# Cross-attention and feed-forward on one core: another order for tiles 4 and 5, a bias row fetched ahead, and an opening that works in smaller pieces

## The reference

```python
def fake_quant(x, s, z):
    q = jnp.clip(jnp.round(x / s + z), 0.0, 255.0)
    return (q - z) * s
x = x + jnp.matmul(fake_quant(_layernorm(x), s1, z1), fake_quant(ctx, s2, z2))
y = _layernorm(x)
base = jnp.matmul(y, w) + bias
A_eff = einsum('bn,nri->bri', gate, lora_A); B_eff = einsum('bn,nor->bor', gate, lora_B)
x = x + base + (y A_eff^T) B_eff^T + (y A_shared^T) B_shared^T
```

## Time and profile before

| what | value |
|---|---|
| runs | 1049.28, 1049.54 and 4784.78 us, median 1049.54 |
| profiled execution | 1046.42 us, its span 1044.9 us |
| PE busy | 991.1 us, 95% of the span |
| DVE, ACT, POOL busy | 536.2, 297.0, 209.8 us |
| granted TensorE clock, mean | 0.996 |
| first product of PE | 15.1 us after the start |

### The profile page before, as it was taken

The page is one execution under the profiler, slowest core; times in us unless marked ns, Lnnn a source line. Parts: engine busy times, 40 slices in busy tenths (PEclk is TensorE's granted clock), DMA queues, the critical chain, the costliest instruction groups (busy, mean ns, idle before and its releaser), DMA issues.

```text
span 1044.9 us, 12005 instructions
## 1 busy us (share of the span) xinstructions
PE 991.1 (95%) x4663; PEld 460.3 (44%) x4663; DVE 536.2 (51%) x756; ACT 297.0 (28%) x213; POOL 209.8 (20%) x233
## 2 busy tenths in 40 slices
PE   2898999898999999999999999998999999999996
PEld 1343444353544444444444444444554444444442
DVE  7766858968554565553423765877542032014010
ACT  4663422253131142232214521363230021012000
POOL 3001100021113013212411643320104004004010
PEclk9999999999999999999999999999999999999999
DMA  8699982859655346446699851767824024014010
GB/s 364 240 307 380 355 306 39 186 115 216 172 183 198 123 152 200 158 149 206 233 294 284 323 204 71 160 123 151 211 107 156 31 101 161 20 40 150 10 50 20
DMA packets 139863, 181.43 MB, mean 174 GB/s; under 512 B 112688, under 2 KB 112688, under 8 KB 127280
## 3 DMA queue, kind: packets, MB, share of 16 engines
q1 hardware_dynamic: 125040, 117.99, 39.1%
q0 software_dynamic: 13632, 58.73, 15.5%
q10 hardware_dynamic: 1152, 4.19, 1.0%
HBM read 124.26 MB, written 29.36 MB: 147 GB/s over the span
## 4 chain that ended last, share of the span: by engine, by line
PE 71%; DVE 10%; DMA 6%; ACT 5%; issue 4%; SPq 1%; POOL 1%; POOLq 0%; ACTq 0%; DVEq 0%
PE psum L1005 17%; PE psum L1187 16%; PE psum L1188 16%; PE psum L1189 16%; PE psum L1210 2%; DVE ring L1446 2%; DMA stage<-in_ctx_in 1%; PE psum L1067 1%; DVE hl L1492 1%; ACT ring L785 1%; DMA bias_sb<-in_bias 1%; DMA xn<-in_x 1%; DMA stage<-in_w 1%; PE psum L1199 1%; PE psum L1198 1%
## 5 line engine op out<-in xcount | busy, mean ns | idle before, releaser
L1187 PE MATMUL psum<-ring,lhs 128*128 128x512 f16 x1016 | 385.8, 380 | 12.6 <-issue 8.5
L1188 PE MATMUL psum<-ring,lhs 128*128 128x512 f16 x1016 | 385.8, 380 | 0.0
L1189 PE MATMUL psum<-ring,lhs 128*128 128x512 f16 x1016 | 385.6, 380 | 0.0
L1005 PE MATMUL psum<-ring,lhs 128*128 128x512 bf16 x1024 | 227.8, 381 | 3.6 <-DVE ring L1412 2.1
L1187 PEld LDWEIGHTS psum<-ring,lhs 128*128 128x128 f16 x1016 | 99.5, 98 | 135.2 <-issue 11.0
L1005 PEld LDWEIGHTS psum<-ring,lhs 128*128 128x128 bf16 x1024 | 100.3, 98 | 126.0 <-issue 4.2
L1189 PEld LDWEIGHTS psum<-ring,lhs 128*128 128x128 f16 x1016 | 99.6, 98 | 120.3 <-issue 0.8
L1188 PEld LDWEIGHTS psum<-ring,lhs 128*128 128x128 f16 x1016 | 99.5, 98 | 118.5 <-issue 0.5
L1499 DVE SCALAR_TENSOR_TENSOR x<-psum,sc,x 128x512 f32<-128x512 f32 (+1 forms) x64 | 45.2, 746 | 191.2 <-PE psum L1199 190.4
L649 POOL TENSOR_TENSOR x<-x,bias_sb 128x512 f32<-128x512 f32 (+1 forms) x64 | 86.6, 1377 | 190.9 <-ACT x L916 130.4
L785 ACT ACTIVATE ring<-stage,sc 128x2048 f16<-128x2048 f32 x32 | 63.6, 1999 | 170.1 <-PE psum L1189 137.8
(11 more groups left out here) (168 smaller groups left out, 656.5 us busy)
## 6 DMA issues: line engine op xcount, KB each, us to landing
stage<-in_w SPq DMA_DIRECT2D x38, 1024.0 KB, 6.3
stage<-in_ctx_in SPq DMA_DIRECT2D x30, 1024.0 KB, 8.1
out<-x POOLq DMA_DIRECT2D x64, 256.0 KB, 3.2
x<-in_x POOLq DMA_DIRECT2D x8, 1024.0 KB, 11.9
xn<-in_x POOLq DMA_DIRECT2D x8, 1024.0 KB, 6.8
x<-in_x POOLq DMA_DIRECT2D x4, 2048.0 KB, 14.7
lhs<-in_lora_a POOLq DMA_DIRECT2D x4, 1024.0 KB, 12.0
lhs<-in_lora_b SPq DMA_DIRECT2D x4, 1024.0 KB, 9.7
```

The lines of the kernel that those rows point to most:

```text
L1005: last = pe.matmul(psum[:, t, :], lhs_q[:, k, t * P:(t + 1) * P], ring_q[:, g, j % 2, u, :], start=(k == 0), stop=(k == KT - 1 and not by_pe))
L1187: pe.matmul(psum[:, t, :], hi, ring[:, g, 0, u, :], start=(kk == 0), stop=False)
L1188: pe.matmul(psum[:, t, :], hi, ring[:, g, 1, u, :], start=False, stop=False)
L1189: last = pe.matmul(psum[:, t, :], lo, ring[:, g, 0, u, :], start=False, stop=False)
```

## The change

In the opening:
- tile 0 of `x` is loaded in two halves with a semaphore each, DVE takes its statistics after each half, ACT scales it in two halves and DVE clips it in two, and PE may turn the first half before the second is clipped;
- group 0 of `ctx` is loaded by POOL between tiles 1 and 2 of `x`, no longer by SP;
- tiles 2 and 3 get their scale one by one (`scale_row`, five DVE instructions, one less than before), where they were a pair;
- the lists of DVE, ACT and PE are written anew: PE starts group 0 of tile 0 before it turns tile 1, and the first column term comes after tile 5, no longer after tile 4.

In the second phase, block 0:
- SP transposes both parts of tile 1 ahead of the load of group 2 of `w`;
- PE takes the products with the high part of group 2 of `w` for tiles 0 and 1 first (`top_group`), which need ACT's work alone, and then the rest (`rest_group`); ACT converts group 2 ahead of the root of tile 2;
- `product_p(b, 0)` and the two `b_pair` stand in front of tile 5, no longer of tile 4, on DVE and ACT; SP transposes tile 5 ahead of `load_a(b, 2)`.

The bias: each block's row is loaded at the end of the addition before it.

```diff
-            load_ctx(0, 0, [0, 1])
+            load_ctx(0, 0, [1])
...
-                        turn_high(b, 1)
-                    if g == 2 and isinstance(j, int) and j == 0:
-                        turn_low(b, 1)
+                        turn_y(b, 1)
...
                 if b == 0:
                     w_peaks_block(1)
+                turn_y(b, 5)
                 load_a(b, 2)
-                turn_y(b, 5)
...
-            load_x(range(4))
+            pool.dma_start(x2[:, 0, 0:D // 2], x_tile[0, 0, :, 0:D // 2]).then_inc(x_half, 16)
+            pool.dma_start(x2[:, 0, D // 2:D], x_tile[0, 0, :, D // 2:D]).then_inc(x_in[0], 16)
+            load_x([1])
+            pool.dma_start(stage[:, 0, :, :], ctx_v[0, 0, 0]).then_inc(first_in, 16)
+            load_x([2, 3])
...
             load_x(range(4, TILES))
-            root_pair(1)
+            root_one(2)
+            root_one(3)
...
+            def next_bias(j, bb):
+                pool.wait_ge(biased, (bb + 1) * TILES)
+                pool.sem_inc(go, 1)
+                pool.dma_start(bias_sb[:, :], bias_row[:, bass.ds(j * NW + NW, NW)].to_broadcast([P, NW])).then_inc(bias_in, 16)
...
                     add_bias(b, j, j + blk2(b, 0), True)
+                    next_bias(j, j + blk2(b, 0))
...
-            relu_rows(0)
-            relu_rows(1)
+            relu_half(0)
+            relu_half(1)
             turn_out(0, range(2))
             ctx_block(0, 0, [0])
+            relu_rows(1)
+            ctx_block(0, 0, [1])
             turn_out(1, range(2))
-            ctx_block(0, 0, [1])
             relu_rows(2)
+            conv_head(2)
             relu_rows(3)
             turn_out(2, [0])
-            conv_head(2)
+            conv_head(3)
             turn_out(3, [0])
-            conv_head(3)
...
+                w_groups(b, 0, [2])
                 root(b, 1, 2)
-                w_groups(b, 0, [2, 3])
+                w_groups(b, 0, [3])
...
                 norm2_rows(3)
+                norm2_rows(4)
                 product_p(b, 0)
                 b_groups(b, 0)
...
             def first_block():
                 turn(0)
+                ring_ready(0, 0, 0)
+                tile_start(0, 0, 0)
+                group1(0, 0, 0, True)
                 turn(1)
+                ring_ready(0, 0, 1)
+                group1(0, 0, 1, True)
+                tile_start(0, 0, 1)
+                for g in range(2):
+                    group1(0, 1, g, True)
                 turn(2)
+                ring_ready(0, 0, 2)
+                for t in range(2):
+                    group1(0, t, 2, True)
+                tile_start(0, 0, 2)
+                for g in range(3):
+                    group1(0, 2, g, True)
                 turn(3)
+                tile_start(0, 0, 3)
+                for g in range(3):
+                    group1(0, 3, g, True)
+                ring_ready(0, 0, 3)
+                for t in range(PT):
+                    group1(0, t, 3, True)
...
# DVE's list of the opening, new
+            stats1(0, range(2)); stats1(0, range(2, NBLK)); variance([0]); scale_row(0)
+            stats1(1, range(2)); round_half(0); stats1(1, [2]); round_half(1); stats1(1, [3]); variance([1])
+            stats1(2, range(2)); scale_row(1); stats1(2, range(2, NBLK)); ctx_group(0, 0, 0); variance([2])
+            round1(1); stats1(3, range(2)); ctx_group(0, 0, 1); scale_row(2); stats1(3, range(2, NBLK)); variance([3])
+            round1(2); scale_row(3); head_group(2); stats1(4, range(1)); turn_out(2); round1(3)
+            stats1(4, range(1, NBLK)); head_group(3); turn_out(3); stats1(5); variance([4, 5])
             scale_rows([4, 5]); stats1(6, range(2)); round1(4); ...
...
                 for t in range(3, TILES):
-                    if t == 4:
+                    if t == 5:
                         product_p(b, 0)
                         for h in range(2):
                             b_pair(b, 0, h)
```

More of the change, by code:

```diff
@@ L682, in _ @@
                     largest(4, MX_W, PW_W)
+                next_bias(0, blk2(b, 0))
                 store(b, 0, blk(b, 1, 0))
@@ L1172, in high_group, with top_group, rest_group @@
                     pe.matmul(psum[:, t, :], hi, ring[:, g, 0, u, :], start=(kk == 0), stop=False)
+                    pe.matmul(psum[:, t, :], hi, ring[:, g, 1, u, :], start=False, stop=False)
+            def top_group(t, g):
+                for u in range(GU):
+                    for h in range(2):
+                        y = lhs[:, h, g * GU + u, t * P:(t + 1) * P]
+                        pe.matmul(psum[:, t, :], y, ring[:, g, 0, u, :], start=False, stop=False)
+            def rest_group(t, g):
+                for u in range(GU):
+                    hi = lhs[:, 0, g * GU + u, t * P:(t + 1) * P]
                     pe.matmul(psum[:, t, :], hi, ring[:, g, 1, u, :], start=False, stop=False)
@@ L1244, in base0_pair @@
                     base_group(1, 1)
[L1245 to L1248 removed]
+                    pe.wait_ge(act_conv, act_w(b, 0, 2) + 1)
+                    for t in range(2):
+                        top_group(t, 2)
+                    pe.wait_ge(converted, grp_w(b, 0, 2) + 1)
+                    for t in range(2):
+                        rest_group(t, 2)
+                    pe.wait_ge(converted, grp_w(b, 0, 3) + 1)
+                    for t in range(2):
+                        base_group(t, 3)
                 def base0(t):
@@ L1354, in stats1 @@
             def stats1(t, parts=range(NBLK)):
-                dve.wait_ge(x_in[t], 16)
+                if t == 0 and 0 in parts:
+                    dve.wait_ge(x_half, 16)
+                else:
+                    dve.wait_ge(x_in[t], 16)
                 for c in parts:
@@ L1382, in scale_rows, with scale_row, round_half @@
                 dve.wait_ge(normed, n + 1)
+            def scale_row(t):
+                i = t % 2
+                root, veps, t2, scale, shift = [v[:, i:i + 1] for v in (
+                    ROOT2, VEPS2, T2, pair_cols(SCALE1, t // 2), pair_cols(SHIFT1, t // 2))]
+                dve.wait_ge(pair_var, t + 1)
+                dve.wait_ge(pair_root, t + 1)
+                then(dve.scalar_tensor_tensor(out=t2, in0=root, scalar=root, in1=veps, op0=ALU.mult, op1=ALU.mult))
+                then(dve.tensor_scalar(t2, t2, 0.5, -1.5, ALU.mult, ALU.add))
+                then(dve.scalar_tensor_tensor(out=t2, in0=root, scalar=IS1, in1=t2, op0=ALU.mult, op1=ALU.mult))
+                dve.tensor_scalar(scale, t2, -1.0, None, ALU.mult)
+                dve.tensor_scalar(shift, MV2[:, i:i + 1, 0], t2, Z1, ALU.mult, ALU.add).then_inc(normed, 1)
+                dve.wait_ge(normed, t + 1)
+            def round_half(h):
+                cols = slice(h * D // 2, (h + 1) * D // 2)
+                dve.wait_ge(relued if h else half_relued, 1)
+                dve.tensor_scalar(q_slots[0][:, cols], q_ints[0][:, cols], 255.0, -CENTRE,
+                                  ALU.min, ALU.add).then_inc(rounded if h else half_rounded, 1)
             def round1(t):
@@ L1690, in _ @@
             lora_pattern()
-            stats1(0)
+            stats1(0, range(2))
+            stats1(0, range(2, NBLK))
             variance([0])
+            scale_row(0)
             stats1(1, range(2))
-            scale_rows([0], 0)
-            stats1(1, range(2, NBLK))
+            round_half(0)
+            stats1(1, [2])
+            round_half(1)
+            stats1(1, [3])
             variance([1])
-            round1(0)
             stats1(2, range(2))
-            scale_rows([1], 1)
+            scale_row(1)
             stats1(2, range(2, NBLK))
+            ctx_group(0, 0, 0)
+            variance([2])
             round1(1)
-            stats1(3)
-            variance([2, 3])
-            ctx_group(0, 0, 0)
-            scale_rows([2, 3], 2)
+            stats1(3, range(2))
             ctx_group(0, 0, 1)
-            stats1(4)
+            scale_row(2)
+            stats1(3, range(2, NBLK))
+            variance([3])
             round1(2)
+            scale_row(3)
+            head_group(2)
+            stats1(4, range(1))
+            turn_out(2)
             round1(3)
-            stats1(5, range(2))
-            turn_out(2)
-            stats1(5, range(2, NBLK))
+            stats1(4, range(1, NBLK))
+            head_group(3)
+            turn_out(3)
+            stats1(5)
             variance([4, 5])
-            head_group(2)
-            turn_out(3)
-            scale_rows([4, 5], 3)
-            head_group(3)
+            scale_rows([4, 5], 4)
             stats1(6, range(2))
```

76 lines of the change are left out of this document (39 added, 37 removed).

## The result

The kernel before took 1050.73 us (median of 5 runs beside it), the changed one 1044.66 us (median of 5): ratio 0.9944, 95% interval 0.9926 to 0.9961, or 5.9 us less. One of the five runs before, 4784.78 us, is far off all the others, and the ratio leaves it out. The forecast was 1038.2 and 11.3 us less. So the time lies in the range and in the class "within 2%", but half of the gain is missing.

What follows compares the result with a forecast made beforehand. PE was taken as the bound, busy 991.1 of 1044.9 us, leaving 53.8 us to touch. Terms -6.4 - 3.44 - 0.3 - 2.7 + 1.5 = -11.3 took 1049.54 to 1038.2 us; range 1032 to 1046.

Steps and rivals of the forecast that it cites:

- tiles 4 and 5: Second phase: PE's stops of 2.15, 2.96 and 3.44 us go; batch 0 gains 6.4 including 0.5 elsewhere, batch 1 3.44.
- pair: Tile 1 and group 2 of w: load starts 189.5, lands in 6.3 us; gains 0.5 in batch 0, 0.3 in batch 1.
- bias rows: POOL's additions: rows fetched ahead let the next x load go 7.2 us earlier; gain 2.7 us, at least 0.
- opening: First block: tile 4's products at 50.2 after a 3.7 us stop; cost 1.5 us, bounds gain 3.7 to loss 5.
- next limit: At lora_in(2), DVE emptying bank 0 would hold PE, so batch 0 gains 6.4 us, not 7.3; stop of about 1 us.
- slow products after a stop: After tile 5's stop in batch 0, eight products each 0.21 us slower; 1.7 us to be won with the stop.
- rival C: Second phase: tile 5's transpose late, or group 2 of w landing at 9 us, returns half the gain; 1043 us, 27%.
- with the row already there the additions end at 321: POOL's bias additions, run from 329.61 before, would end at 321 once the row was fetched ahead; part of the 2.7 us.
- the load goes at 332.5, 7.2 us earlier: Load of batch 1's next x tile, before at 339.74; DVE reaches block 2's w groups some 6 us earlier.
- loads behind it: After the opening, ctx, adapter and shared loads issue 3.5 us later; 1.0 us lateness for block 1, bounds 0 and 3.5.
- B: Opening: DVE keeps tiles 4 to 7 in time and 3.7 us stay won; 1033 us, 13%.
- D: Opening: PE's clock stays at the lower level in the first block, ending it 24.7 us later; 1061 us, 3%.

Runs made afterwards that it cites:

- first experiment: Kernel before with only product_p(0) and the two b_pair moved behind tile 4, and tile 5 transposed ahead of load_a(2): ratio 0.9891, 11.5 us less.
- version with all: Changed kernel with the tile 1 and group 2 order as before, small POOL additions, SP waiting for the second x tile, POOL's root covered: 1032.79 us, ratio 0.9837.
- run with the opening: Kernel before with the new order of tiles 4 and 5 and the whole new opening, bias rows as before: ratio 0.9904.
- kernel with both: Kernel before with the new order of tiles 4 and 5, bias rows fetched ahead and small POOL additions in idle stretches: ratio 0.9857.

## Why the prediction was half right

| term | forecast | measured | from |
|---|---|---|---|
| tiles 4 and 5, both batches | -9.3 | -11.5 | first experiment |
| pair, both batches | -0.8 | +3.7 to +4.6 | undone, 0.9909 and 0.9900 for 0.9944 |
| bias rows | -2.7 | +1.8, +1.9 | undone, and alone |
| opening | +1.5 | +1.4 | 0.9904 for 0.9891 |
| sum | -11.3 | -4.6 to -3.6 | the whole change: -5.9 |

The forecast of the first row is 6.4 less the 0.5 of the pair, and 3.44. The parts add up to the whole within what they are known to.

**Tiles 4 and 5** went by the prediction's steps, `lora_in(2)` as the next limit included (a stop of 0.67 in the changed kernel). The median gained 2 us more than was counted, while between the two traces it is 6.4 us, less than was counted. So the 9.3 is borne out by neither, and that it lies between them is in part luck. A part of the gap is the clock: the mean granted clock was 0.992 over the nine runs of the kernel before beside the first experiment, and 0.995 over that one's four. Its profiled execution, on which the sum rests, had 0.996. Over the 31 runs of the kernel before in the three sets, 0.001 of clock goes with about 0.4 us, so by that estimate the 0.003 are worth some 1.2 us. The 1.7 us of slow products after a stop were counted once, after one stop; they come and go from run to run. In the first experiment's trace they stand behind the stop of 2.52 us at tile 1, eight products 0.43 us apart from 197.5 us on, so there the 1.7 us were not won but moved. The row of the version with all shows such a case (1.89 us where 1.04 stands in the earlier trace rows for the same four products), and so does PE at 90 us: 8.83 us for 16 products of float32 in the run with the opening, 7.13 in the changed kernel. The rest of the gap between the medians and the traces stays open.

**The pair** is the step that failed first. The prediction had the load of group 2 go out at 189.5 and land in 6.3 us; it went out at 190.92, since the transpose ahead of it took 3.42 us to issue, and landed in 6.0. So the landing time was right and the issue of the transpose was mis-sized, at some 2 us. DVE's two splits then began at 198.97 and 203.44, so the second ended at 205.8, not 204.35. `top_group` doesn't hide it: PE had run out of products 1.49 us before 205.84. In batch 1 the load went out only 0.7 us later than before (669.28 for 668.54) but next to that of group 3, and took 8.8 us: the "9 us" that rival C had for batch 0. There the term should have been priced by what came to lie together (two loads of `w` and a transpose of the adapter matrix within 1.8 us, right behind another transpose), not by the median of 38 loads; which of these neighbours costs how much was not tested.

**The bias rows** failed at the sentence "with the row already there the additions end at 321". The earlier trace rows show 18.76 us "<-issue", and I read them as the wait for the row. They were two waits, one behind the other: the row, 11.9 us from its issue, and then POOL's change from the all-reduce to an addition, 7.4 us; small additions paid 6.7 to 7.7 for it, with little or nothing moving. Only behind the loop did the two pass side by side: in block 3 of the kernel before the additions began at 492.67, as soon as the row was there, 11.03 us after POOL's last issue. With the row fetched ahead only the second is left, but now it falls beside the 1 MB load and two loads of `w`, and there it took 9.1 to 12.6 us. So the additions came 7.0 us earlier after the x load, not at once. The Trainium skill, "GPSIMD Engine Reference", section "2.1 Instruction dispatch", says that the first call of a freshly loaded kernel pays about 6 us for loading code, with no instruction in the profile that shows it; the small additions come near this size, but that POOL loads code here no run shows.

The other way the traces don't agree with one another. In the loop the all-reduce starts 8.4 to 9.2 us after POOL's last issue, 7.3 to 8.1 of them after DVE's value is there. Yet the one at 276.24, behind additions too, starts 0.14 us after DVE's value; there POOL had waited 13.73 us, and whether the change passed in that time, as it seems in block 3, stays open.

But had that been seen, the term would have been wrong still. Everything at this place is 4.73 us earlier than before. The second x load went out 8.47 us earlier, so 3.7 more than that; DVE could use the tile only 4.23 us earlier, so 0.5 less than that, as the load now ran into two loads of `w`. The prediction said "the load goes at 332.5, 7.2 us earlier" and carried the 7.2 us to DVE at the old landing time of 5.7 us. It took 9.9. By the rule of equal turns that the prediction cites from the Trainium skill, "DMA: Bandwidth & Descriptors", it would have finished ahead of the second load of `w`. In the kernel with both it landed with it, at 338.8 us, but not against that rule: once its packets moved it had 51.2% of the engines beside 45.4%, and what the rule doesn't say is that the first of them moved over 4 us after the issue.

**The opening** came out as walked: tile 4's products at 49.57 (50.2 forecast) after a stop of 3.04, and DVE 0.91 us in wait for POOL. Its 1.0 us for the loads behind it is not confirmed by itself: before adapter `b` PE stops 2.08 us for 1.46, which is 0.6, but this stop is 1.5 to 2.3 us in the traces with the old opening and 2.1 to 3.0 in those with the new one. The 1.4 us of the ratios are under their noise; that PE's column sum behind it starts later in all six traces speaks for a cost.

**Rivals.** B is out. C had the right place, `w` group 2, and the wrong half: tile 5's transpose made no trouble. Its time of 1043 is near the 1044.66 measured, but by luck: what was lost went to the pair in both batches and, as far as it can be told, to the bias rows, and not to tile 5. D is out: the page of the changed kernel shows the granted clock in the top tenth in every slice of the opening.

## What to carry to other kernels

A transfer that is let out earlier is only worth its landing time in its new company: look up what else is issued in the 3 us around it, and let the one that is waited for go first, even at the price of a wait on another queue (here 2.7 us for one line). "Idle, <-issue" ahead of an instruction is a question, not a term: look up when the thing that it is said to wait for landed. Here 7.4 of 18.76 us came after that, and a wait that is left can grow when it falls into busier company (12.57 us). And try the parts of a change one by one, because here one part was worth 11.5 us and the other three together cost half of it.

## What the runs showed of the hardware

- POOL's first TENSOR_TENSOR after a PARTITION_ALL_REDUCE starts 6.7 to 7.7 us after POOL's last instruction even for one column, and 9.1 to 12.6 us beside a 1 MB load and other traffic. In the loop this comes on top of a wait for a transfer (7.2 and 7.4 us after the bias row had landed), in block 3 it did not. A small addition in an idle stretch takes this wait: the eight additions behind it start as soon as the load ahead of them is issued.
- Beside POOL's eight additions DVE's SCALAR_TENSOR_TENSOR on 64x1024 took 9.95 us for 1.28, and ended 1.1 us after them. The eight additions took 9.83 us beside it (304 to 314 us), and 11.85 us beside other work of DVE (318 to 330).
- A 1 MB load on POOL's queue landed in 5.7 us beside 0.52 MB of ACT's, and in 10.9 us when there were also 2.10 MB on SP's queue, issued 0.6 us before and 1.5 us after it; its first packet moved about 2 us after the issue in the one case, over 4 us in the other.
